# Batches of 14 tiles instead of 15 in a gather and scatter-add kernel: six pooled tiles in turns of two, 223 steps

## The chip, the cores and the metric

The kernel runs on one core of a Trainium2 chip. The metric is the time of one execution on the device, in microseconds (us). The kernel before took 2930.49 us, the median of three runs (2925.21 to 2933.01).

## The reference

There are 12,500 nodes of 32 features (`x`) and 400,000 edges, each with a source node `src`, a destination node `dst` and 32 features of its own. The edges are sorted by `dst`. All numbers are float32.

```python
def _L0_gnn_ref(node_inputs, edge_inputs, src, dst, W, b, eps):
    msg = jax.nn.relu(node_inputs[src] + edge_inputs)
    agg = jax.ops.segment_sum(msg, dst, num_segments=N_NODES)
    h = (1.0 + eps[0]) * node_inputs + agg
    return h @ W.T + b
x = _layernorm(x + _L0_gnn_ref(x, edge_attr_32, src, dst, L0_gnn_W, L0_gnn_b, L0_gnn_eps), axis=-1)
```

Nearly all the work is the first two lines: fetch a row of `x` for each edge, add, ReLU, and sum by destination.

## The kernel before

**Tiles and batches.** A tile is 128 edges, one on each partition; there are 400,000 / 128 = 3125 tiles. A batch is `TILES` = `LOOK` + `POOLED` = 8 + 7 = 15 tiles. The first batch is a short one of `SHORT` = 3125 mod 15 = 5 tiles, and `ROWS` = 208 full batches follow it, so the main part has 208 equal steps, one for each full batch. It is a software pipeline: in a step each engine works on several batches, some ahead and one behind. Steps -3 to 3 are written out, then a loop of 50 rounds runs over a ring of four buffers, and the last seven steps are written out again. TensorE's program alone has one step in the body of its loop (`steps(pe, step, 1)`).

**Two ways of fetching rows.** In each batch the seven pooled tiles are gathered by GpSimd (POOL), with one indirect DMA of 128 rows of 128 bytes for a tile (L550). The eight looked-up tiles take no gather. For these TensorE multiplies with one-hot matrices, on a copy of `x` that lies in SBUF in three bfloat16 parts. First `look_in_buckets` (L1162, 96 matmuls of 96 columns in a step) builds a small table from up to 57 slots in each of 32 buckets. Then ScalarE (ACT) copies the table out of PSUM (`fill_table`, L971, two halves), and `look_in_table` (L1184 and L1144) multiplies four blocks of 24 matmuls of 128 columns with one-hot matrices of the keys. VectorE (DVE) picks the right quarter of each result (`pick`, L798, four instructions). All this costs the same in each step, whatever number of tiles is pooled.

**What prepares it.** The buckets are ranked on DVE and TensorE (`count_ranks`, L1215 to L1221; `fill_slots`, L1230). ACT copies the slots (L978), SyncE (SP) writes them and the keys to DRAM and loads them again spread over all 128 partitions (456 KB and 256 KB in a step). DVE and ACT make the one-hot matrices from them (L768, L780; L996 and L1003, L1015 and L1021).

**What works on all tiles of a batch.** DVE adds edge features to the fetched rows (`add_rows`, L810), and makes a one-hot matrix of the destinations (`mark_batch`, L813). ACT takes the ReLU (L986). TensorE sums by destination (`sum_batch`, L1194): two instructions for each tile, since the operands are float32. DVE adds two windows of 40 nodes to the sum (L837). SP loads the edge features with two DMAs (112 KB for the pooled part, 128 KB for the looked-up part) and the indices of the pooled tiles with one.

**The turns.** POOL's gathers of a batch are issued in three groups, `TURNS`. The first waits for the end of `look_in_buckets` (semaphore `l1_ready`), the second for two blocks of `look_in_table` (`blocks_looked`) and the third for all four. So the groups are spread over TensorE's step:

```python
if k == 0:
    if not free:
        pool.wait_ge(sums_ready, b - RING + 1)
        pool.wait_ge(l1_ready, (b - RING + 2) * KEYS)
    pool.wait_ge(index_loaded[slot], use * 16 + 16)
elif not free:
    pool.wait_ge(blocks_looked, (b - RING + 1) * KEYS + k * KEYS // 2)
```

`gather` fetches for a batch three steps ahead of the one that DVE adds.

Of the kernel before, what the change touches and what calls it, by code (L numbers as in the profile page):

```python
# [11 lines left out]
def gnn_kernel(nc, x, src, dst, edge, weight, bias, eps, out):  # L12
# [4 lines left out]
    NODES, D = x.shape  # L17
    EDGES = src.shape[0]
    LOOK = 8
    POOLED = 7  # L20
    TILES = LOOK + POOLED
    SHORT = EDGES // P % TILES
    BATCH, FIRST = P * TILES, P * SHORT
# [37 lines left out]
    PAIRS = (TILES + 1) // 2  # L61


    TURNS = [(0, 3), (3, 5), (5, POOLED)]
    EARLY, CHUNK = 8, 72
    HEAD, FROM, TO = 4, -3, ROWS + 3
    ROUNDS = (ROWS - 3 - HEAD) // RING
# [10 lines left out]
    ZRING = 4  # L78
    assert SHORT <= POOLED and WINDOW <= P and LOOK % 2 == 0
    assert EDGES == FIRST + BATCH * ROWS and SHORT > 0 and PAD % CLEARS == 0 and ROUNDS > 0  # L80
# [4 lines left out]
    def spans(values):  # L85

        batches = values[FIRST:].rearrange("(b e) -> b e", e=BATCH)
        return (batches[:, 0:P * POOLED].rearrange("b (p j) -> b p j", j=POOLED),
                batches[:, P * POOLED:BATCH].rearrange("b (p j) -> b p j", j=LOOK))

    src_pooled, src_looked = spans(src)
    dst_spans = spans(dst)
    edge_batches = edge[FIRST:, :].rearrange("(b e) f -> b e f", e=BATCH)
    edge_spans = (edge_batches[:, 0:P * POOLED, :].rearrange("b (p j) f -> b p (j f)", j=POOLED),
                  edge_batches[:, P * POOLED:BATCH, :].rearrange("b (p j) f -> b p (j f)", j=LOOK))
# [24 lines left out]
    with ctx:  # L120
# [424 lines left out]
        def _(pool):  # L545
# [6 lines left out]
            def gather(st):  # L552
                if has(st, 3, BATCHES):
                    b, slot, use = st.s + 3, slot_of(st, 3, RING), uses(st, 3)
                    free = isinstance(b, int) and b < RING
                    for k, (j0, j1) in enumerate(TURNS):
                        if k == 0:
# [761 lines left out]
```

## Time and profile before

| | |
|---|---|
| median of three runs | 2930.49 us |
| the profiled execution | 2931.13 us |
| its span, first to last instruction | 2929.0 us |
| TensorE's mean granted clock, share of full speed | 0.909 |
| busy: PE, DVE, ACT, POOL | 81%, 62%, 56%, 49% |
| DMA, mean over the span | 81 GB/s |
| gathers on POOL | 1461 |

The page gives for each engine the time in which it was busy. For a group of instructions it gives their count, their busy time together, the mean duration of one, and the idle time of the engine just before them with what ended it. "Issue" means that the engine waited for nothing that the profile shows. TensorE overlaps its instructions, so a group's busy time divided by its count is what one adds to the stream, and the mean duration is not.

### The profile page before, as it was taken

The page shows a single profiled execution, that of the slowest core. Times are in us where ns is not written, and L with a number is a line of the kernel's source. Part 1 is how long each engine was busy: PE and PEld are TensorE (multiplying, and loading weights), DVE is VectorE, ACT ScalarE, POOL GpSimd, SP SyncE. Part 2 cuts the span into 40 slices and gives each one's busy share as a digit, 9 for nine tenths or more (in the row PEclk, how much of TensorE's full clock was granted, in tenths as well). Part 3 has the DMA queues.
Part 4 walks back from the last instruction along what each step waited for, and adds up shares of the span by engine and source line. Part 5 has one row for each costly group of instructions (what it writes and reads, how often), then busy time and mean ns, then how long its engine had stood idle before and what let it go on. Part 6 is the DMA issues. An engine that isn't in the chain of part 4 may idle for free. (4 is left out here: it accounts for less than half of the span.)

```text
span 2929.0 us, 110879 instructions
## 1 busy us (share of the span) xinstructions
PE 2382.3 (81%) x49112; PEld 1842.9 (63%) x35800; DVE 1812.9 (62%) x4504; ACT 1635.8 (56%) x1720; POOL 1434.8 (49%) x1467
## 2 busy tenths in 40 slices
PE   4788888888888888788888888888887878888788
PEld 2566666666666666666666666666666666666664
DVE  5766666666666666665665656666666566565665
ACT  4655555555555555555555555555555555555554
POOL 4454545544545454455455445445555545545541
PEclk9988999989989899989999999898899999898988
DMA  5333333333333333333333333333333333333332
GB/s 123 68 86 79 81 81 79 86 76 78 86 77 81 83 76 83 81 79 85 78 78 86 79 76 86 76 84 81 78 86 79 79 82 79 86 79 76 86 79 50
DMA packets 244832, 236.54 MB, mean 81 GB/s; under 512 B 107748, under 2 KB 190750, under 8 KB 244805
## 3 DMA queue, kind: packets, MB, share of 16 engines
q1 hardware_dynamic: 198053, 212.15, 31.1%
q0 software_dynamic: 46752, 24.03, 5.8%
q8 instruction: 17, 0.28, 0.0%
q14 instruction: 10, 0.08, 0.0%
HBM read 233.21 MB, written 2.78 MB: 81 GB/s over the span
## 5 line engine op out<-in xcount | busy, mean ns | idle before, releaser
L550 POOL DMA_INDIRECT rows_all<-in_x,index x1461 | 1434.3, 982 | 1442.6 <-PE l L1162 611.9
L1144 PE MATMUL found<-table,oh 128*128 128x128 bf16 x13312 | 1288.3, 227 | 12.7 <-issue 11.9
L1184 PE MATMUL found<-table,oh 128*128 128x128 bf16 x6656 | 1271.7, 233 | 21.2 <-issue 12.8
L1184 PEld LDWEIGHTS found<-table,oh 128*128 128x128 bf16 x6656 | 928.3, 139 | 335.8 <-issue 122.5
L1162 PE MATMUL l<-xparts,oh 128*57 128x96 bf16 x19968 | 717.0, 225 | 434.3 <-issue 434.2
L1162 PEld LDWEIGHTS l<-xparts,oh 128*57 128x57 bf16 x19968 | 590.8, 121 | 560.0 <-issue 559.2
L798 DVE COPY_PREDICATED rows_all<-mask,found 128x256 f32<-128x256 uint16 x832 | 370.3, 445 | 657.5 <-PE found L1144 507.0
L971 ACT CAST table<-l 128x768 bf16<-128x768 f32 x416 | 330.3, 795 | 661.7 <-PE l L1162 632.4
L780 DVE TENSOR_SCALAR oh<-keys,lanes 128x1024 bf16<-128x1024 f16 x624 | 295.6, 489 | 190.9 <-PE found L1144 139.8
L1015 ACT ACTIVATE oh<-keys,minus_lanes 128x1024 bf16<-128x1024 f16 x208 | 238.9, 1148 | 264.6 <-PE found L1144 222.1
L996 ACT ACTIVATE oh<-slots,minus_lanes 128x1824 bf16<-128x1824 f16 x208 | 375.2, 1804 | 6.8 <-DMA slots<-slot_dram 6.8
L1003 ACT ACTIVATE oh<-oh 128x1824 bf16<-128x1824 bf16 x208 | 357.3, 1718 | 0.0
L768 DVE TENSOR_SCALAR oh<-slots,lanes 128x1824 bf16<-128x1824 f16 x416 | 277.7, 709 | 115.5 <-issue 75.2
L1021 ACT ACTIVATE oh<-oh 128x1024 bf16<-128x1024 bf16 x208 | 220.7, 1061 | 0.0
L1194 PE MATMUL win<-onehots,relus 128*32 128x40 f32 x6250 | 201.0, 225 | 21.9 <-issue 19.5
L1194 PEld LDWEIGHTS win<-onehots,relus 128*32 128x32 f32 x6250 | 173.7, 131 | 52.1 <-issue 30.1
L978 ACT CAST slot_row<-ranks 32x57 f16<-32x57 f32 x208 | 41.4, 199 | 293.4 <-PE ranks L1230 206.7
L813 DVE TENSOR_TENSOR onehots<-win,rel 128x600 f32<-128x600 f32 (+1 forms) x209 | 161.5, 773 | 5.9 <-PE win L1194 2.0
L810 DVE TENSOR_TENSOR msg<-rows_all,msg 128x480 f32<-128x480 f32 (+1 forms) x209 | 136.0, 651 | 0.1
L986 ACT ACTIVATE relus<-msg 128x480 f32<-128x480 f32 (+1 forms) x209 | 124.0, 593 | 16.3 <-DVE msg L810 16.3
L759 DVE TENSOR_TENSOR in_slot<-ranks,bucket 128x456 f16<-128x456 f32 x208 | 129.6, 623 | 0.0
L747 DVE TENSOR_TENSOR placed<-ob,src_sb 128x256 f16<-128x256 f16 x208 | 88.6, 426 | 41.8 <-DVE counts L731 22.7
(127 smaller groups left out, 1031.0 us busy)
## 6 DMA issues: line engine op xcount, KB each, us to landing
slots<-slot_dram SPq DMA_DIRECT2D x208, 456.0 KB
keys<-key_dram SPq DMA_DIRECT2D x208, 256.0 KB
msg<-in_edge SPq DMA_DIRECT2D x208, 128.0 KB
rows_all<-in_x,index POOLq DMA_INDIRECT x1461
msg<-in_edge SPq DMA_DIRECT2D x208, 112.0 KB
index<-in_src SPq DMA_DIRECT2D x208, 3.5 KB
key_dram<-key SPq DMA_DIRECT2D x208, 2.0 KB
slot_dram<-slot_row SPq DMA_DIRECT2D x208, 3.6 KB
```

Of the source, the lines that this page charges most:

```text
L550: pool.indirect_dma_start(to, None, x, bass.IndirectOffsetOnAxis(indices[:, j:j + 1], 0)).then_inc(done, 16)
L768: nc.vector.tensor_scalar(oh1[:, j, :], slots[:, two, :], lanes[:, j:j + 1], None, ALU.is_equal).then_inc(oh1_ready, 1)
L780: nc.vector.tensor_scalar(key_marks(b), by_edge(keys[:, four, :]), lanes[:, b:b + 1], None, ALU.is_equal).then_inc(oh2_ready, 1)
L798: nc.vector.copy_predicated(rows[slot][:, POOLED * D:ROW].rearrange("p (t f) -> p t f", f=D), mask[:, two, :, k:k + 1].bitcast(U16).to_bro ...
L971: nc.scalar.copy(table[:, some, :], l1_all[:, :].rearrange("p (k c) -> p k c", k=KEYS)[:, some, 0:PARTS * FOUND]).then_inc(table_ready, 1)
L996: nc.scalar.activation(oh1[:, DVE_SUBS, :], slots[:, two, :], ACT.Square, bias=minus_lanes[:, DVE_SUBS:DVE_SUBS + 1]).then_inc(slots_squar ...
L1003: nc.scalar.activation(at, at, ACT.Relu, scale=-2.0, bias=1.0).then_inc(oh1_act_ready, 1)
L1015: nc.scalar.activation(key_marks(b), by_edge(keys[:, four, :]), ACT.Square, bias=minus_lanes[:, b:b + 1]).then_inc(keys_squared, 1)
L1144: return nc.tensor.add_instruction(mybir.InstMatmult(name=nc.get_next_instruction_name(), engine=mybir.EngineType.PE, ldweights=False, ins ...
L1162: last = nc.tensor.matmul(l1_of(g)[half * HALF:half * HALF + CAP, :, :], oh1[:, j, b * CAP:(b + 1) * CAP], xparts[:, j * EVEN + b, :, :], ...
L1184: last = nc.tensor.matmul(to, key_marks(b)[:, :, t], part, start=begin, stop=end, skip_group_check=True)
L1194: last = nc.tensor.matmul(win_sums(g), relus[:, tiles[j], :], onehots[:, tiles[j], :], start=(j == 0), stop=(j == len(tiles) - 1))
```

## The change

`POOLED` becomes 6, so a batch has 14 tiles. 3125 mod 14 is 3, so the short batch has 3 tiles, and there are 3122 / 14 = 223 full batches. The turns become two, two and two gathers. Everything else follows from these numbers: 54 rounds of the loop in place of 50, six written-out steps at the end in place of seven, 95 batches in the second half of 128 partitions in place of 80 (so that their tables of indices load with two DMAs in place of one), and tables of 223 columns in place of 208.

```diff
@@ -17,7 +17,7 @@
     NODES, D = x.shape
     EDGES = src.shape[0]
     LOOK = 8
-    POOLED = 7
+    POOLED = 6
     TILES = LOOK + POOLED
     SHORT = EDGES // P % TILES
     BATCH, FIRST = P * TILES, P * SHORT
@@ -61,7 +61,7 @@
     PAIRS = (TILES + 1) // 2
 
 
-    TURNS = [(0, 3), (3, 5), (5, POOLED)]
+    TURNS = [(0, 2), (2, 4), (4, POOLED)]
     EARLY, CHUNK = 8, 72
     HEAD, FROM, TO = 4, -3, ROWS + 3
     ROUNDS = (ROWS - 3 - HEAD) // RING
```

## Rows read from the trace of the kernel before

**Rows 1.** The page's first part: busy time, share and instructions of each engine
```profile
PE 2382.3 (81%) x49112; PEld 1842.9 (63%) x35800; DVE 1812.9 (62%) x4504; ACT 1635.8 (56%) x1720; POOL 1434.8 (49%) x1467
```
**Rows 2.** The line of ACT's slot copy, once in a step, from 400 to 2640 us
```profile
L978 ACT CAST slot_row<-ranks x165: 183/200/203, 404.3 to 2639.3; 32x57 f16<-32x57 f32 x165
```
**Rows 3.** Waits of PE, POOL and DVE, 400 to 2640 us: us, times, longest
```profile
PE l L1162 <- issue: 340.6, 615, 1.2
PE win L1194 <- issue: 13.2, 29, 0.5
...
PE ranks L1215 <- ACT slot_row L978: 9.1, 28, 0.9
...
POOL rows_all L550 <- PE l L1162: 486.4, 160, 4.6
POOL rows_all L550 <- PE found L1144: 321.6, 200, 2.3
POOL rows_all L550 <- issue: 269.8, 769, 1.9
...
DVE rows_all L798 <- PE found L1144: 405.6, 153, 4.7
```
**Rows 4.** Groups by line: count, busy us, mean ns of one, idle before
```profile
L550 POOL DMA_INDIRECT rows_all<-in_x,index x1461 | 1434.3, 982 | 1442.6 <-PE l L1162 611.9 <-PE found L1144 423.2 <-issue 348.2
...
L1162 PE MATMUL l<-xparts,oh 128*57 128x96 bf16 x19968 | 717.0, 225 | 434.3 <-issue 434.2
...
L1194 PE MATMUL win<-onehots,relus 128*32 128x40 f32 x6250 | 201.0, 225 | 21.9 <-issue 19.5 <-DVE aggX L837 1.6
```
**Rows 5.** The lines that work on all tiles, by form, 400 to 2640 us
```profile
L813 DVE TENSOR_TENSOR onehots<-win,rel 128x600 f32<-128x600 f32 x165 | 127.7, 774 | 3.7 <-PE win L1194 1.3
L810 DVE TENSOR_TENSOR msg<-rows_all,msg 128x480 f32<-128x480 f32 x164 | 107.0, 652 | 0.0
L986 ACT ACTIVATE relus<-msg 128x480 f32<-128x480 f32 x165 | 98.1, 595 | 0.0
```
**Rows 6.** The same lines on the short batch of five tiles
```profile
L813 DVE TENSOR_TENSOR onehots<-win,rel 128x200 f32<-128x200 f32 x1 | 0.4, 358 | 0.0
L986 ACT ACTIVATE relus<-msg 128x160 f32<-128x160 f32 x1 | 0.3, 337 | 0.6 <-DVE msg L810 0.6
L810 DVE TENSOR_TENSOR msg<-rows_all,msg 128x160 f32<-128x160 f32 x1 | 0.3, 321 | 0.0
```
**Rows 7.** POOL's timeline over one step: start us, duration, idle before and releaser
```profile
1545.93 0.94 POOL L550 DMA_INDIRECT rows_all<-in_x,index  x1 [1.96 <-PE l L1162]
1547.18 1.26 POOL L550 DMA_INDIRECT rows_all<-in_x,index  x1 [0.30 <-issue]
1548.75 1.00 POOL L550 DMA_INDIRECT rows_all<-in_x,index  x1 [0.30 <-issue]
1551.21 0.94 POOL L550 DMA_INDIRECT rows_all<-in_x,index  x1 [1.47 <-PE found L1144]
1552.46 0.95 POOL L550 DMA_INDIRECT rows_all<-in_x,index  x1 [0.30 <-issue]
1554.89 0.95 POOL L550 DMA_INDIRECT rows_all<-in_x,index  x1 [1.49 <-PE found L1144]
1556.14 0.94 POOL L550 DMA_INDIRECT rows_all<-in_x,index  x1 [0.30 <-issue]
```
**Rows 8.** PE's timeline from 1512.3 us: the bucket phase of one step
```profile
1512.36 0.95 PE L1162 MATMUL l<-xparts,oh 128*57 128x96 bf16 x35
1513.74 0.25 PE L1162 MATMUL l<-xparts,oh 128*57 128x96 bf16 x2 [0.42 <-issue]
1514.50 0.26 PE L1162 MATMUL l<-xparts,oh 128*57 128x96 bf16 x3 [0.51 <-issue]
...
1516.75 1.27 PE L1162 MATMUL l<-xparts,oh 128*57 128x96 bf16 x50 [0.49 <-issue]
```
**Rows 9.** Stages of 2 us, all engines: busy, granted clock, DMA share, GB/s
```profile
1500.00:1502.00 2.00, 0.81 (x9) 0.47 (x10) 1.50 (x5) 0.00 (x0) 1.43 (x2) 0.92 0.31 80
1502.00:1504.00 2.00, 1.57 (x41) 1.52 (x40) 1.80 (x6) 0.80 (x1) 0.00 (x0) 0.50 0.05 8
...
1514.00:1516.00 2.00, 0.55 (x7) 0.31 (x8) 1.50 (x5) 0.20 (x1) 1.66 (x2) 1.00 0.60 194
```
**Rows 10.** Spans and granted clock of the core
```profile
core 0: 2929.0 us, clock 0.909
```
**Rows 11.** DMA queues over the span: packets, MB, share of 16 engines
```profile
q1 hardware_dynamic: 198053, 212.15, 31.1%
q0 software_dynamic: 46752, 24.03, 5.8%
```

## The prediction

> **What bounds the kernel now.** I read the busy times first [rows 1]. TensorE is busy 81% of the span, DVE 62%, ACT 56% and POOL 49%, so POOL, the engine whose work the change reduces, is the least loaded of the four. The reader should not stop there, since the gathers are issued in turns and could still end a wait.
>
> Next I measured the step. ACT's slot copy runs once in each; 165 of them start between 404.3 and 2639.3 us [rows 2], so a step takes 2235.0 / 164 = 13.63 us. The profiled execution took 2931.13 us, 0.6 us over the median, and 208 steps make 2835.0 us of it. The fixed part (start, filling and draining of the pipeline, the output) is 2931.13 - 2835.0 = 96.1 us.
>
> Third, the waits [rows 3], over those 164 steps. TensorE waits for other engines hardly at all: 9.1 us for ACT's slot copy. Its large loss is 340.6 us (2.08 us a step) in `look_in_buckets` with no releaser in the profile. In the timeline it is a run of matmuls that breaks after 35, then goes on with two to four at a time with 0.42 to 0.51 us between, and then runs freely again [rows 8]. No engine waits for a gather: DVE's `add_rows`, the one reader of gathered rows, sits idle 0.0 us before its 164 instructions [rows 5]. It is POOL that waits for TensorE, 486.4 us for the end of the buckets and 321.6 us for the table blocks [rows 3]. DVE's `pick` also waits for TensorE (405.6 us). So TensorE's own stream with its breaks sets the step, and its clock is part of it: the granted clock is 0.909 on average [rows 10], which with the two levels of 1.2 and 2.4 GHz means that 2 x (1 - 0.909) = 18% of the span, 533 us, ran at the low one. The fall comes behind a break: from 1500 to 1502 us TensorE was busy 0.81 of 2 us, and in the next 2 us the clock was 0.50 [rows 9].
>
> **The change part by part.** *Steps.* 208 become 223. The table, the picks, the ranks, the one-hots and the two spread loads don't depend on the number of pooled tiles, so fifteen more of each run. At today's step that is 15 x 13.63 = +204.5 us. Against it stands what a step saves, 223 times. The break-even saving is 204.5 / 223 = 0.92 us a step.
>
> *One tile less to sum on TensorE.* Two of the 30 L1194 instructions go. They add 201.0 / 6250 = 0.032 us each [rows 4], so 0.064 us a step, on the path. By mean duration (225 ns each, not overlapped) it would be 0.45 us. I take 0.064, since the neighbours overlap.
>
> *One gather less on POOL.* It goes from the first turn and frees 0.98 us busy [rows 4] and the 0.30 us before it [rows 7], 1.28 us a step. In the step shown, the third gather starts at 1548.75 and ends at 1549.75; the second turn starts at 1551.21, after 1.47 us of waiting for TensorE's table blocks. Without the gather POOL waits longer, and the four later gathers stay where they are. So I cost it at nothing. If POOL were the bound, it would be worth the whole 1.28 us (rival B).
>
> *Smaller operands.* Between the 5-tile and the 15-tile form L813 goes from 358 to 774 ns, L810 from 321 to 652, and L986 from 337 to 595 [rows 5, 6]. One tile is thus 42 + 33 = 75 ns on DVE and 26 ns on ACT. Both engines wait for TensorE within the step, so this is hidden; its bounds are 0 and 0.10 us.
>
> *Transfers.* A step loads 16 KB less of edge features and gathers 16 KB less. By the queues' shares [rows 11] the gathers cost 5.8% of 2929 us / 1461 = 0.12 us of all sixteen engines each. The other queue moves 212.15 MB in 31.1% (911 us), 4.3 us a MB, so 16 KB are 0.07 us. Together this is 0.19 us of a DMA time of 36.9% of 13.63 = 5.0 us. If TensorE's breaks lie behind transfers (from 1514 to 1516 us it was busy 0.55 of 2 us while 194 GB/s moved [rows 9]), some of it may come back. But the loads in that stretch are the spread slots and keys and the third turn, of which nothing is removed. Bounds: 0 to 0.19 us; I take 0.04.
>
> *Sum for a step.* 0.064 + 0.04 = 0.10 us, so 13.53 us. For the unknowns (breaks, clock phase) I keep a saving between -0.20 and +0.40 us. The reason for either end is the clock: steps alternate with and without a stretch at the low level, and a shift by a tenth of a microsecond can make such stretches come more or less often. All of them together cost at most half of 533 us over 208 steps, 1.28 us a step; a quarter more or fewer is about 0.3 us.
>
> *Fixed part.* The second half of the index tables loads with two DMAs, 95 rows are turned instead of 80, and the last chunk of the source descriptions has 71 columns instead of 56. I take +2 us, with 0 and 5 as bounds, giving 98 us. The short batch of three tiles in place of five changes tenths.
>
> Forecast: 98 + 223 x 13.53 = 3115 us, 6.3% slower.
>
> One rule speaks on the breaks. The timeline shows each bucket phase breaking off with nothing in the profile to release it, some 1 us after the loop's new step began [rows 8]. The Trainium skill (Runtime: NRT & Kernel Launch, Instruction fetch mechanics) says that a taken branch to a page outside the two held ones makes the engine fetch it before it goes on. By that rule the loss belongs to the loop's round, one round to a step, and comes fifteen times more often, with nothing saved per tile; that is already the forecast. If instead the loss went with the tiles, it would shrink by 1/15 of 2.08, 0.14 us a step, and the time would be 3084 us, inside the range.
>
> **The rivals.** *A. The breaks or the low clock get rarer or more frequent.* For it: the clock is a large term, 1.28 us a step at most, and it hangs on the phase of the breaks. Against a large shift: what makes the breaks stays in each step. A saving of 0.40 gives 98 + 223 x 13.23 = 3048 us; a loss of 0.20 gives 3182 us.
>
> *B. POOL's gathers set the step after all.* Then the step falls by 1.28 us, to 12.35, and the time is 98 + 2754 = 2852 us, 2.7% faster. This is the rival on the other side. Its place is the third turn, which runs while the buckets do, and it decides from a saving of 0.92 us. Against it: POOL idles 1442.6 us [rows 4] and is released by TensorE in nearly all turns, and `add_rows` never waits for rows [rows 5].
>
> *C. The clock stays high.* If the breaks moved so that the low level never came, a step would save 1.28 + 0.10 us, giving 98 + 223 x 12.25 = 2830 us, faster. It needs 72% of the low stretches to go before the kernel is even (0.92 of 1.28). Nothing in the change touches the third turn and the spread loads, with which the breaks coincide in time. The Trainium skill (TensorE: Matmul & The Clock Gate, Part 1) says that the clock follows how busy the array was; the rows agree (0.81 of 2 us busy, then 0.50). By that rule breaks that remain keep the low stretches.
>
> *D. The change saves nothing at all in a step, because TensorE is released once a step by something of fixed pace.* Then 98 + 223 x 13.63 = 3137 us.
>
> **How the numbers follow.** Forecast with its spread of some 35 us to both sides: 0.72. D, 3137, lies in the same range: 0.10. A beyond 3060 downwards: 0.06; A beyond 3165 upwards: 0.07. B: 0.02. C, or any mixture that gets below 2922: 0.03. A measurement of this kernel can tell about 0.3% (9 us) from no change. The range is 3060 to 3165: the forecast, D and the nearer parts of A. Faster by over 0.3%: 0.04. Within 0.3%: 0.01. Slower by over 0.3%: 0.95.
>
> **What would show it.** Right: ACT's slot copies 13.4 to 13.65 us apart; 223 x 6 + 3 = 1341 gathers; L1162's idle time per step still 2.0 to 2.2 us; POOL's idle time in a step longer by about 1.2 us, under the releasers of now; L1194 with 28 instructions a step at 0.032 us each; the clock between 0.90 and 0.92. Wrong: a step under 13.2 us. If POOL's waits shrink in it, B holds; if the clock is over 0.95, C does. If L1162's breaks are much shorter though four gathers stand where they stood, then the removed gather or the smaller loads fed them. A step over 13.8 us with a lower clock is A's slow side.

## The result and the profile after

The kernel after took 2759.2 us, the median of four runs (2750.2 to 2760.14), against 2929.66 us before: a ratio of 0.941, 95% interval [0.939, 0.943]. It is 5.9% faster, where 6.3% slower was forecast, and the time lies far outside the range of 3060 to 3165 us. Fifteen more steps did come, but each step became 1.7 us shorter, where 0.1 was forecast.

The lines of the kernel after that answer to the rows of before. First busy time and instructions by engine, and the groups of gathers, bucket matmuls and sums (count, busy us, mean ns | idle us before and releaser):

```profile
PE 2377.5 (86%) x52185; PEld 1853.9 (67%) x37913; DVE 1937.4 (70%) x4819; ACT 1736.6 (63%) x1839; POOL 1325.7 (48%) x1347
...
L550 POOL DMA_INDIRECT rows_all<-in_x,index x1341 | 1325.2, 988 | 1381.8 <-PE found L1144 724.5
...
L1162 PE MATMUL l<-xparts,oh 128*57 128x96 bf16 x21408 | 643.2, 208 | 290.1 <-issue 289.2
...
L1194 PE MATMUL win<-onehots,relus 128*32 128x40 f32 x6250 | 190.3, 207 | 38.6 <-issue 36.9
```

TensorE's busy time is what it was [rows 1], in a span shorter by 171 us. Fifteen more steps run in it, but a bucket matmul takes 208 ns in the mean in place of 225, which fits the shorter time at the low clock that is worked out below. The idle time in the bucket phase fell from 434.3 us in 208 steps to 290.1 us in 223 [rows 4], 2.09 to 1.30 us a step.

The slot copy, once a step, from 400 to 2640 us, and then the waits of the same stretch:

```profile
L978 ACT CAST slot_row<-ranks x188: 197/199/203, 403.2 to 2629.9; 32x57 f16<-32x57 f32 x188
```
```profile
POOL rows_all L550 <- PE found L1144: 604.6, 374, 3.0
DVE rows_all L798 <- PE found L1144: 377.6, 188, 3.4
...
POOL rows_all L550 <- PE l L1162: 320.9, 171, 3.9
PE l L1162 <- issue: 238.4, 481, 0.5
...
PE ranks L1215 <- ACT slot_row L978: 3.3, 12, 0.4
```

A step takes (2629.9 - 403.2) / 187 = 11.91 us, against 13.63 [rows 2]. The core's line gives the granted clock, 0.958 against 0.909 [rows 10]:

```profile
core 0: 2758.3 us, clock 0.958
```

So the low level held for 2 x 0.042 x 2758 = 232 us in place of 533.

Where a step's time went can be read from the starts of TensorE's phases. This table is worked out from all of TensorE's matmul starts in the steady part (mean us of a phase):

```
                bucket  sum   table 1-2  fill  table 3  ranks  table 4   step
before           5.52  0.95   3.22       0.36  1.75     0.33   1.51     13.6
after            4.23  0.85   3.26       0.34  1.45     0.33   1.48     11.9
```

Of the 1.7 us, 1.29 came in the bucket phase, 0.30 in the third table block, and 0.10 in the sum. In the third block the matmul behind the slot copy (L1215) starts within 0.16 us of the end of that copy in 45% of the steps before and in 6% of them after, so some of these 0.30 us are a wait for it; the rows of waits name it for only 9.1 and 3.3 us in all.

The mechanism is seen when POOL's and TensorE's timelines are laid side by side. Before, POOL from 1505 to 1516 us; the bucket phase of this step starts at 1512.36 [rows 8]:

```profile
1505.69 1.26 POOL L550 DMA_INDIRECT rows_all<-in_x,index  x1 [3.96 <-PE l L1162]
1507.25 0.95 POOL L550 DMA_INDIRECT rows_all<-in_x,index  x1 [0.30 <-issue]
1508.51 0.95 POOL L550 DMA_INDIRECT rows_all<-in_x,index  x1 [0.31 <-issue]
1510.89 0.95 POOL L550 DMA_INDIRECT rows_all<-in_x,index  x1 [1.44 <-PE found L1144]
1512.14 0.95 POOL L550 DMA_INDIRECT rows_all<-in_x,index  x1 [0.30 <-issue]
1513.77 0.95 POOL L550 DMA_INDIRECT rows_all<-in_x,index  x1 [0.68 <-issue]
1515.02 0.94 POOL L550 DMA_INDIRECT rows_all<-in_x,index  x1 [0.30 <-issue]
```

After, POOL from 1509 us, and TensorE from 1512 us:

```profile
1509.41 1.10 POOL L550 DMA_INDIRECT rows_all<-in_x,index  x1 [2.76 <-PE found L1144]
1510.82 0.95 POOL L550 DMA_INDIRECT rows_all<-in_x,index  x1 [0.30 <-issue]
1513.16 0.95 POOL L550 DMA_INDIRECT rows_all<-in_x,index  x1 [1.40 <-PE found L1144]
1514.41 0.95 POOL L550 DMA_INDIRECT rows_all<-in_x,index  x1 [0.30 <-issue]
```
```profile
1512.10 1.91 PE L1162 MATMUL l<-xparts,oh 128*57 128x96 bf16 x79
1514.49 0.29 PE L1162 MATMUL l<-xparts,oh 128*57 128x96 bf16 x3 [0.49 <-issue]
1515.27 0.24 PE L1162 MATMUL l<-xparts,oh 128*57 128x96 bf16 x2 [0.49 <-issue]
1516.01 0.47 PE L1162 MATMUL l<-xparts,oh 128*57 128x96 bf16 x12 [0.49 <-issue]
```

Before, the second turn is released late, its second gather (1512.14 to 1513.09) reaches into the bucket phase, and with the two of the third turn three gathers lie beside it. TensorE breaks off after 35 matmuls and needs 5.7 us. After, the second turn is over at 1511.77, before the phase starts; only two gathers lie beside it. TensorE breaks off after 79 matmuls and needs 4.4 us. Over all steady steps, the second turn is over before the phase, or at most 0.35 us into it, in 36% of the steps before and in 94% after.

### The profile page after: what moved, and what is told of

It reads as the page before. It is cut to its first block and busy times, and to the rows that moved or that the text cites. A ratio compares the mean times of both kernels' runs of the same rounds, so it can differ in the third digit from the quotient of the medians.

```text
span 2758.3 us, 117759 instructions
## 1 busy us (share of the span) xinstructions
PE 2377.5 (86%) x52185; PEld 1853.9 (67%) x37913; DVE 1937.4 (70%) x4819; ACT 1736.6 (63%) x1839; POOL 1325.7 (48%) x1347
## 5 line engine op out<-in xcount | busy, mean ns | idle before, releaser
L550 POOL DMA_INDIRECT rows_all<-in_x,index x1341 | 1325.2, 988 | 1381.8 <-PE found L1144 724.5
L1144 PE MATMUL found<-table,oh 128*128 128x128 bf16 x14272 | 1374.8, 227 | 0.9
L1184 PE MATMUL found<-table,oh 128*128 128x128 bf16 x7136 | 1362.2, 233 | 8.8 <-DVE rows_all L798 6.6
L1184 PEld LDWEIGHTS found<-table,oh 128*128 128x128 bf16 x7136 | 995.8, 140 | 319.8 <-issue 92.5
L1162 PE MATMUL l<-xparts,oh 128*57 128x96 bf16 x21408 | 643.2, 208 | 290.1 <-issue 289.2
L1162 PEld LDWEIGHTS l<-xparts,oh 128*57 128x57 bf16 x21408 | 535.4, 108 | 394.7 <-issue 387.8
L798 DVE COPY_PREDICATED rows_all<-mask,found 128x256 f32<-128x256 uint16 x892 | 398.5, 447 | 548.5 <-PE found L1144 442.6
L768 DVE TENSOR_SCALAR oh<-slots,lanes 128x1824 bf16<-128x1824 f16 x446 | 305.9, 726 | 114.3 <-issue 111.7
L1194 PE MATMUL win<-onehots,relus 128*32 128x40 f32 x6250 | 190.3, 207 | 38.6 <-issue 36.9
L1194 PEld LDWEIGHTS win<-onehots,relus 128*32 128x32 f32 x6250 | 162.1, 115 | 74.1 <-issue 56.9
L813 DVE TENSOR_TENSOR onehots<-win,rel 128x560 f32<-128x560 f32 (+1 forms) x224 | 163.0, 728 | 1.3 <-issue 1.3
L986 ACT ACTIVATE relus<-msg 128x448 f32<-128x448 f32 (+1 forms) x224 | 127.1, 567 | 18.3 <-DVE msg L810 17.0
L810 DVE TENSOR_TENSOR msg<-rows_all,msg 128x448 f32<-128x448 f32 (+1 forms) x224 | 138.3, 617 | 0.1
```

Of the source, the lines that this page charges most:

```text
L550: pool.indirect_dma_start(to, None, x, bass.IndirectOffsetOnAxis(indices[:, j:j + 1], 0)).then_inc(done, 16)
L768: nc.vector.tensor_scalar(oh1[:, j, :], slots[:, two, :], lanes[:, j:j + 1], None, ALU.is_equal).then_inc(oh1_ready, 1)
L798: nc.vector.copy_predicated(rows[slot][:, POOLED * D:ROW].rearrange("p (t f) -> p t f", f=D), mask[:, two, :, k:k + 1].bitcast(U16).to_bro ...
L1144: return nc.tensor.add_instruction(mybir.InstMatmult(name=nc.get_next_instruction_name(), engine=mybir.EngineType.PE, ldweights=False, ins ...
L1162: last = nc.tensor.matmul(l1_of(g)[half * HALF:half * HALF + CAP, :, :], oh1[:, j, b * CAP:(b + 1) * CAP], xparts[:, j * EVEN + b, :, :], ...
L1184: last = nc.tensor.matmul(to, key_marks(b)[:, :, t], part, start=begin, stop=end, skip_group_check=True)
```

## The experiments

Theory G: gathers (indirect DMAs of POOL) beside the bucket phase break TensorE's stream, and the seventh gather costs the step by that. The rivals: the change in size does it (S), or the breaks come from the loop's new round or from the spread loads (F). The kernels of one group ran on one chip together with the kernel before, and all ratios are against that. The groups ran on different chips, which mattered: the kernel before took 2930 us on the chip of the result, 2868 and 2867 us in the first and third group, and 2166, 2165 and 2165 us in the second, fourth and fifth. The expectations in us for chips with breaks were set from the 2930 us of the first chip, so on the others the step and the ratio are what can be compared.

### First group (before: 2868 us): the seventh gather alone, and where it lies

`b6`, the kernel before without the third gather of the first turn. It does not fetch the rows of that tile, so its output is wrong and only its time counts:

```diff
 for j in range(j0, ...):
+    if j == 2 and not (isinstance(b, int) and b == 0):
+        continue
     gather_tile(rows[slot][:, j * D:(j + 1) * D], index[slot], j, rows_gathered[slot])
```

> The kernel before with 208 steps and 15 tiles, but the third gather of the first turn is not issued (tile 2 of each full batch keeps zeros in place of its rows), so that six gathers are left in turns of two, two and two; all other instructions and loads stay. Theory G (the seventh gather itself costs the step 1.6 us): 12.0 us a step, some 2595 us, clock near 0.95. Theory S (the smaller operands and edge loads, or TensorE's shorter stream, shift the step): 13.6 us a step, some 2930 us.

Measured: 2522.76 us, ratio 0.880 [0.870, 0.890], 11.69 us a step. One gather less, with all other instructions of a step as they were, took (2868.3 - 2522.8) / 208 = 1.66 us from each step.

`a7`, the kernel after with a seventh gather:

```diff
+if k == 0 and not (isinstance(b, int) and b == 0):
+    gather_tile(spare[:, slot * D:(slot + 1) * D], index[slot], 0, rows_gathered[slot])
```

> The kernel after with 223 steps and 14 tiles, and one more gather at the end of the first turn, into a buffer that nobody reads. Theory G: the step goes back to 13.5 to 13.7 us, some 3110 to 3150 us, clock near 0.91. Theory S: 11.9 to 12.0 us a step, some 2760 us.

Measured: 3070.19 us, ratio 1.071 [1.068, 1.074], 13.34 us a step. This is what the forecast described (1.063): 223 steps at the old length, which was 13.31 us in `before2` on a chip as fast as this one. The bucket group in it (L1165 here) has its breaks back, 2.0 us a step:

```profile
L1165 PE MATMUL l<-xparts,oh 128*57 128x96 bf16 x21408 | 761.1, 222 | 441.0 <-issue 440.4
```

Theory S falls with both. `b223` and `b232` move the gather:

```diff
-    TURNS = [(0, 3), (3, 5), (5, POOLED)]
+    TURNS = [(0, 2), (2, 4), (4, POOLED)]   # b223
+    TURNS = [(0, 2), (2, 5), (5, POOLED)]   # b232
```

> The kernel before with turns of 2, 2 and 3 gathers in place of 3, 2 and 2. If the count of gathers decides (theory G): 13.6 us a step, 2930 us. If it is the third gather of the first turn, by where it lies: some 12 to 12.5 us, 2600 to 2700 us. If gathers that lie beside the bucket phase break TensorE's stream there: slower than before, 14.3 us and 3070 us.

> The kernel before with turns of 2, 3 and 2 gathers. If the count decides: 2930 us. If the third gather of the first turn does, by its place: 2600 to 2700 us. If the third turn is pushed later by the longer second one and its gathers then lie outside the bucket phase: a little faster than before, with fewer breaks in that phase.

Measured: `b223` 3089.21 us, ratio 1.078 [1.074, 1.081], 14.40 us a step; `b232` 2840.84 us, ratio 0.989 [0.986, 0.993]. The count is seven in both, so the place decides too: `b223` is 8% slower than the kernel before, not equal to it, as by the count, nor faster, as by the third gather of the first turn alone. With three gathers in the third turn, all three lie beside the bucket phase in every step, and its idle time is 2.5 us a step; with the third one in the second turn it is 1.8 us:

```profile
L1162 PE MATMUL l<-xparts,oh 128*57 128x96 bf16 x19968 | 701.2, 213 | 512.3 <-issue 512.3
```
```profile
L1162 PE MATMUL l<-xparts,oh 128*57 128x96 bf16 x19968 | 676.3, 213 | 374.4 <-issue 369.5
```

### Second group (before: 2166 us): a chip without breaks

> The kernel before with 208 steps and 15 tiles, but without the third gather of the first turn and without both gathers of the third turn, so that four are left, none of them beside the bucket phase (tiles 2, 5 and 6 of a full batch keep zeros in place of their rows). Theory G (each gather takes some 1.2 us from TensorE where it falls in the bucket phase): the bucket phase falls from 4.1 us with six gathers to 2.3 us or less, the breaks go, and a step takes 9.9 to 10.3 us, 2160 to 2240 us. Theory F (the breaks come from the loop's new round or from the spread loads of slots and keys): the bucket phase keeps breaks of 1 us or more, a step of 11.5 us, 2490 us.

> The kernel after with one pooled tile less again: five gathers in turns of two, two and one, 13 tiles, 240 steps. Theory G: the one gather less beside the bucket phase saves 1.2 us there, a step of 10.7 us, 98 + 240 x 10.7 = 2666 us, faster than the kernel after. If TensorE's own work is the floor by now: 11.4 us a step, 2834 us, slower than the kernel after.

> The kernel after, with four short iotas on POOL (no DMA) in the place of the seventh gather, at the end of the first turn. If a gather harms by its transfers: 11.9 us a step as the kernel after, 2700 to 2760 us. If it harms by keeping POOL busy, so that the second turn comes late or the SBUF port is held: 13.0 us a step or more, 3000 us or more.

> The kernel after, with one more load a step from the SP queue right behind the edge loads: 128 rows of 128 bytes, as many rows and bytes as a gather fetches, but no work for POOL. If any small transfer harms as a gather does: 13.3 us a step, 3070 us. If it takes a transfer issued by POOL: 11.9 to 12.1 us, 2700 to 2800 us.

`b4` skips j = 2, 5 and 6 as `b6` does j = 2, and its output is wrong in the same way. `c5` is the kernel after with `POOLED = 5`; it also needs `CHUNK = 78` in place of 72 and one more small copy on VectorE while it prepares. `p1` and `p2` are the kernel after with one thing more in a step: `p1` has four iotas (short instructions on POOL without a DMA) where the seventh gather was, `p2` a load on SP:

```diff
+for again in range(4):                                              # p1, on POOL
+    nc.gpsimd.iota(spare[:, again * 112:(again + 1) * 112], ...)
+sp.dma_start(spare[:, slot * D:(slot + 1) * D], x[...][:, 0, :])    # p2, on SP
```

On this chip none of these four kernels had a break, and all expectations for chips with breaks went untested. `b4` took 2145.47 us (0.990 [0.988, 0.993]), `p1` 2302.24 (1.063), `p2` 2279.94 (1.053), `c5` 2422.20 us (1.118 [1.115, 1.121]). Here three gathers less are worth 21 us in all, 0.1 us a step, and fewer tiles a step lose what more steps cost. The bucket group of `p2` shows the phase whole, with at least one gather beside it in every step (L1164 here):

```profile
L1164 PE MATMUL l<-xparts,oh 128*57 128x96 bf16 x21408 | 499.0, 207 | 1.2 <-ACT oh L1005 0.9 <-issue 0.3
```

Four iotas have a mean of 297 ns, so `p1` keeps POOL as busy as a gather would; without breaks this costs 22 us more than `p2`.

### Third group (before: 2867 us): a chip with breaks again

> The kernel before once more, for its profile on the chip of this call, since it took 2930, 2868 and 2166 us on three chips. If the chip is like that of 2166 us: a bucket phase of 2.2 us without breaks and a step of 9.95 us, 2166 us. If like the others: a bucket phase of 5.1 to 5.5 us with breaks and a step of 13.3 to 13.6 us.

> The kernel after on the same chip. Theory G says that the change gains only where gathers break TensorE's stream: on a chip without breaks a step saves 0.1 to 0.2 us and the kernel is slower by 5 to 6% (2275 to 2300 us against 2166); on a chip with breaks it is faster by 4 to 6%.

> The kernel before without the third gather of the first turn and without the third turn (four gathers a step, 208 steps; tiles 2, 5 and 6 of a full batch keep zeros for their rows). On a chip with breaks, theory G: the bucket phase falls to some 2.2 to 2.5 us and the step to 9.9 to 10.3 us, 2160 to 2240 us; theory F (the breaks belong to the loop's round or to the spread loads): breaks of 1 us or more stay and the step is 11.5 us. On a chip without breaks: 2145 us as measured.

> The kernel after with its six gathers in two turns of three, so that none is issued for the bucket phase. On a chip with breaks, theory G: one gather of the second turn at most reaches into the bucket phase, which falls from 4.2 to some 2.5 to 3.2 us; a step of 10.7 to 11.5 us, 2480 to 2660 us, unless gathers cost the same beside the table phase (then 11.9 us and 2760 us). On a chip without breaks: the same as the kernel after within 1%.

`a33` is `TURNS = [(0, 3), (3, 6)]` on the kernel after. Measured: `before2` 2865.33 us (1.000); `after2` 2701.7 us, ratio 0.943 [0.935, 0.952]; `a33` 2710.5 us (0.947); and `b4_again` 2155.54 us, ratio 0.753. That last is the strongest result here. The chip that takes 2867 us for the kernel before takes 2156 us once the third turn and the third gather are gone, within 0.5% of `b4` on the chip without breaks. A step takes 9.86 us, just under the 9.9 to 10.3 us that theory G expected. Its bucket group, one bucket phase, and its clock:

```profile
L1168 PE MATMUL l<-xparts,oh 128*57 128x96 bf16 x19968 | 468.4, 207 | 6.7 <-issue 6.5
```
```profile
1500.11 2.23 PE L1168 MATMUL l<-xparts,oh 128*57 128x96 bf16 x96
```
```profile
core 0: 2154.8 us, clock 0.994
```

All 96 matmuls run through in 2.2 us, with idle time of 6.7 us in the whole run instead of 434.3 [rows 4]. Its loop rounds and its spread loads are those of the kernel before, so theory F falls: neither breaks the stream by itself. That gathers do it only together with the spread loads, which lie beside the same phase, is not excluded.

`a33` missed its expectation (11.70 us a step, not 10.7 to 11.5). I had thought one gather would reach into the bucket phase. Its second turn came as late as in the kernel before, 2.5 us behind the end of the second table block, and put two there; the phase took 4.11 us. Its clock was 0.996, so these breaks did not bring the low level. In return its third table block took 0.4 us longer than that of `after2`: L1215 starts within 0.16 us of the end of the slot copy in 97% of its steps, against 6% in `after2`, which points to a wait for that copy.

Grouping all steady steps of the eight kernels that ran on chips with breaks (and `before` and `after` themselves) by the number of gathers that start from 0.5 us before the bucket phase to 0.8 us before its end gives the price:

```
gathers beside the phase          0      1      2      3      4
median bucket phase, us         2.16   2.99   4.23   5.84   7.83
steps                            181     50    992    627     12
```

Each gather adds 0.8 to 2.0 us; the ends of the table rest on few steps. The count is taken over the phase itself, so a phase that is long for another reason takes in more gathers. Kernels in which all steps have the same count are free of that, and agree: a mean of 2.17 us with none (`b4_again`), 4.11 with two (`a33`), 5.74 with three (`b223`). The kernel before has three in 59% of its steps and two in 40%; the kernel after has two in 89%.

### Fourth and fifth group (before: 2165 us)

> The kernel after with four short iotas on POOL in the place of the seventh gather (no DMA). On a chip with breaks: 11.7 to 11.9 us a step (2700 to 2760 us) if a gather harms by its transfer, 13.0 us or more if by keeping POOL busy. On a chip without breaks: 2302 us as measured.

> The kernel after with one more load of 128 rows of 128 bytes a step from the SP queue behind the edge loads. On a chip with breaks: 13.3 us a step (3070 us) if any small transfer harms, 11.7 to 12.1 us (2700 to 2800 us) if it takes a transfer issued by POOL. On a chip without breaks: 2280 us as measured.

> The kernel after with its six gathers in one turn behind the bucket phase. Six gathers 1.25 us apart take 7.5 us, as long as the sum and table phases (7.6 us), so only the last can touch the next bucket phase. On a chip with breaks: 10.0 to 10.6 us a step, 2330 to 2460 us, if the place decides; 11.7 us, 2700 us, if the count does. On a chip without breaks: 2280 us.

> The kernel before with its seven gathers in one turn behind the bucket phase, which take 8.75 us, so the last falls beside the next bucket phase and breaks it once. On a chip with breaks: 10.8 to 11.5 us a step, 2340 to 2490 us, if the place decides; 13.3 us, 2865 us, if the count does. On a chip without breaks: 2166 us.

Both groups ran on chips without breaks, the fifth with repeats, `b7_one_turn_2` and `p1_third`, so the expectations for chips with breaks went untested again. The times: `p1_again` 2303.16 and `p1_third` 2302.47 us; `p2_again` 2280.51 us; `a6_one_turn` 2284.51 us, ratio 1.055 [1.052, 1.058]; `b7_one_turn` 2155.96 us, ratio 0.996 [0.994, 0.998], and 2156.49 in its repeat, also 0.996. One turn of seven (`TURNS = [(0, POOLED)]`) is thus 0.4% faster than the kernel before on such a chip and the fastest kernel that computes everything; how it does on a chip with breaks wasn't measured. Whether a gather's transfer or POOL's occupation does the harm, for which `p1` and `p2` were made, is not settled either.

## Why the prediction was wrong

**What was read rightly.** TensorE's stream sets the step, no one waits for a gather, and the breaks and the low clock are large terms. The fixed part was forecast as 98 us and came to 2760.14 - 223 x 11.91 = 104. The terms for smaller work were small, as forecast: L1194 adds 190.3 / 6250 = 0.030 us an instruction, and of the 1.7 us a step only some 0.05 are left once the gather's 1.66 (`b6`, on another chip) are taken off, beside the 0.10 I summed. Where TensorE has no breaks the sum fits. The step of one turn of seven with 15 tiles takes 9.90 us there, that of one turn of six with 14 tiles 9.80, and the latter kernel takes 6.0% longer (2284.51 against 2155.96 us), against the 6.3% forecast. The kernel after itself was not run on such a chip, so that it would lose some 5% there is inferred from `a6_one_turn` and `p2`.

**The step that failed** is the term "One gather less on POOL", of which the prediction says "So I cost it at nothing". It is worth 1.66 us a step (`b6`). I took the nothing from the one step in [rows 7], where the second turn is over before the bucket phase. In most steps it is not: in 59% of them three gathers lie beside the phase. I had a row of such a step beside me, the bucket phase from 1512.36 us [rows 8], and didn't lay POOL's timeline along it. The released engine was the one I looked at; the work that the gather disturbs while it runs has no releaser in the profile and shows as "issue". I also claimed that the four later gathers "stay where they are". They came earlier: the second turn starts 0.8 us after the end of the second table block, for which it waits, in the step shown of after (1509.41), and 2.4 us after it in the one shown of before (1510.89). The medians are 2.3 to 2.5 us in `before`, `a7` and `a33`, each with three gathers in the first turn, and 0.8 to 1.2 us in `after`, `b6`, `b223` and `b232` with two. The semaphore events of the traces show where the time goes: in the step of after the block ends at 1508.61 and its increment comes at 1508.62; in the step of before the block ends at 1508.49 and the increment comes at 1510.10. POOL's gather starts 0.8 us behind the increment in both. So TensorE's release comes late behind a third gather. Why it does is not shown. I had also expected POOL to idle 1.2 us longer in a step; it idled 1442.6 / 208 = 6.9 us before and 1381.8 / 223 = 6.2 us after.

**The bounds.** I put a ceiling of 0.40 us on the saving from the clock alone, and held in rival A that "what makes the breaks stays in each step". I had weighed transfers, loop rounds and clock phase as their causes, but gave the seventh gather's reach into that phase no rival and no price. It stands only among the signs of being wrong: much shorter breaks "though four gathers stand where they stood" would mean that "the removed gather or the smaller loads fed them". `b6` and `a7` show that it was the gather, and the four had moved. Rival A named the right stretch with a price of 0.40 us, a quarter of what came; C was right that the clock would rise (0.909 to 0.958) and too small in weight. The clock's share can be bounded: the low level held 2.56 us a step before and 1.04 after, so at most 0.76 of the 1.7 us. In the kernel before, a low stretch begins in 81% of the steps with three gathers beside the phase and in 25% of those with two. But `a33`, with two in every step, has none in its steady part, so the count does not fix the clock by itself. The prediction's working has a slip in C as well: since 0.10 us are saved in any case, 64% of the low stretches had to go for break-even (0.82 of 1.28), not 72%. B named the right sign for the wrong reason: POOL still waits for TensorE.

**The rule.** By the Trainium skill (Runtime: NRT & Kernel Launch, Instruction fetch mechanics), I laid the breaks to the taken branch of each round. `b4_again` takes the same branches and has no breaks, so the measurement decides against that reading here. The trace of before could have told it. Its DMA queues have these packets of instructions in the whole run, and of 400 to 2640 us, with 164 rounds in it, the same view lists none:

```profile
q8 instruction: 17, 0.28, 0.0%
q14 instruction: 10, 0.08, 0.0%
```

So no load of instructions shows in the steady rounds, and the condition of the rule, a target outside the held pages, is not seen there.

## What to carry to other kernels

An idle time put down to "issue" has a cause as well: lay the timelines of all engines along it, in several steps of each kind and not in one, and ask what runs at the time. An asynchronous helper that no one waits for can still cost the busiest engine more than its own duration, here 1.66 us a step for a gather of 0.98 us. When a loss of that kind comes and goes with the chip, a tuned size may hold only for the chips that have it.

## What the runs showed of the hardware

The same program took from 2165 to 2930 us on different chips. On some, POOL's gathers beside a dense run of small matmuls break that run; on others they do not: `b7_one_turn`, with the same work and one or two gathers beside the run in each step, has a mean of 2.16 us there. The kernel before itself has no trace on such a chip, so that its run is whole there is inferred. Where the gathers do harm, the run of 96 matmuls of 2.16 us grows to 2.99, 4.23, 5.84 and 7.83 us with one to four gathers beside it. The granted clock of these traces was 0.859 to 0.946 with seven gathers a step, 0.958 to 0.996 with six, and 0.994 with four that lie elsewhere. Beside the table blocks, turns of two gathers cost nothing that shows: `b4_again` takes 9.86 us a step with them and `b4` takes 9.85 on a chip without breaks. The matmuls of the table are wider, and SP's loads are denser beside the bucket phase (some 190 against 75 GB/s in `b4_again`); whether either matters was not tested. Why some chips have these breaks and others have none stays open.
